# Causal attention on one core: weighing with float32 probabilities and values instead of split float16 ones

## The reference

```python
qkv = x @ W_qkv
q, k, v = jnp.split(qkv, 3, axis=-1)
q, k, v = (to_heads(q), to_heads(k), to_heads(v))      # 16 heads of 64
q, k = (apply_rope(q), apply_rope(k))
dots = jnp.einsum('bhid,bhjd->bhij', q, k) * scale
dots = jnp.where(causal, neg, dots)
attn = jax.nn.softmax(dots, axis=-1)
out = jnp.einsum('bhij,bhjd->bhid', attn, v)            # "weighing"
out = out.transpose(0, 2, 1, 3).reshape(b, n, INNER)
out = jax.nn.relu(out @ W_o1) @ W_o2
...
```

## Time and profile before

| | us |
|---|---|
| median of three runs | 5071.18 |
| profiled execution, its time | 5068.41 |
| profiled execution, its span | 5066.7 |
| `attention_heads`: stretch before the first turn | 2616 to 2722 |
| 15 turns with all side jobs (pairs 0 to 14) | 2722 to 4471 |
| last turn | 4471 to 4560 |
| both `attention_out` | 4560 to 4660 |

### The profile page before, as it was taken

The page is one execution under the profiler, slowest core; times in us unless marked ns, Lnnn a source line. Parts: engine busy times, 40 slices in busy tenths (PEclk is TensorE's granted clock), DMA queues, the critical chain, the costliest instruction groups (busy, mean ns, idle before and its releaser), DMA issues. The chain is left out here.

```text
span 5066.7 us, 84689 instructions
## 1 busy us (share of the span) xinstructions
PE 3697.3 (73%) x28907; PEld 2605.5 (51%) x28907; DVE 3704.5 (73%) x4463; ACT 2570.4 (51%) x4134; POOL 2389.1 (47%) x1532
## 2 busy tenths in 40 slices
PE   2997645555555569948936998999989898994595
PEld 1663224444434446637813665666656565663484
DVE  6993579999999989930067888888888888885101
ACT  1222456666666632222214676777767676784221
POOL 0220268888888832220034666656656666600202
PEclk9998767777777789959958999999999999996697
DMA  2000001001101000024532222222222222202254
GB/s 86 0 0 4 7 21 32 30 29 30 31 29 29 30 28 0 0 96 153 162 118 55 55 54 48 47 49 68 52 64 53 52 53 54 52 10 91 73 181 155
DMA packets 236314, 276.23 MB, mean 55 GB/s; under 512 B 63820, under 2 KB 183557, under 8 KB 234561
## 3 DMA queue, kind: packets, MB, share of 16 engines
q1 hardware_dynamic: 223056, 244.85, 17.8%
q0 software_dynamic: 8704, 24.35, 1.4%
q10 hardware_dynamic: 4224, 2.76, 0.2%
HBM read 152.60 MB, written 36.04 MB: 37 GB/s over the span
## 5 line engine op out<-in xcount | busy, mean ns | idle before, releaser
L2247 DVE TENSOR_TENSOR att_b_prob_low<-att_b_prob,att_b_prob_high 128x1024 f16<-128x1024 f32 (+2 forms) x640 | 780.4, 1220 | 64.0 <-ACT att_b_prob_high L2214 55.2
L2274 DVE TENSOR_REDUCE att_b_neg_max<-att_b_peek 128x1 f32<-128x1024 f32 (+1 forms) x748 | 667.8, 906 | 143.1 <-PE att_b_peek L2102 115.8
L2212 ACT ACTIVATE att_b_prob<-att_b_score,att_soft 128x1024 f32<-128x1024 f32 (+2 forms) x640 | 633.7, 990 | 219.9 <-PE att_b_score L2125 145.7
L1030 PE MATMUL mix_scan_hT<-ident,mix_scan_h 128*128 128x128 f32 x1024 | 248.7, 389 | 536.1 <-DVE mix_scan_h L978 502.1
L2214 ACT ACTIVATE att_b_prob_high<-att_b_score,att_soft 128x1024 f16<-128x1024 f32 (+2 forms) x640 | 630.8, 986 | 10.1 <-PE att_b_o L2153 3.6
L1030 PEld LDWEIGHTS mix_scan_hT<-ident,mix_scan_h 128*128 128x128 f32 x1024 | 172.5, 197 | 650.7 <-DVE mix_scan_h L978 443.9
L2149 PE MATMUL att_b_o<-att_b_vh,att_b_prob_high 128*128 128x65 f16 x4352 | 464.4, 195 | 36.9 <-DVE att_b_prob_low L2247 27.5
L2123 PE MATMUL att_b_score<-att_b_q_both,att_b_k_twice 128*128 128x512 f16 (+3 forms) x1280 | 450.5, 352 | 31.4 <-ACT att_b_prob_high L2214 21.9
L2149 PEld LDWEIGHTS att_b_o<-att_b_vh,att_b_prob_high 128*128 128x128 f16 x4352 | 402.4, 98 | 128.8 <-DVE att_b_prob_low L2247 73.5
L2153 PE MATMUL att_b_o<-att_b_vh,att_b_prob_low 128*128 128x65 f16 x4352 | 463.2, 194 | 0.0
L2151 PE MATMUL att_b_o<-att_b_vl,att_b_prob_high 128*128 128x64 f16 x4352 | 462.7, 193 | 0.0
(11 more groups left out here) (344 smaller groups left out, 9612.7 us busy)
## 6 DMA issues: line engine op xcount, KB each, us to landing
moe_w<-in_L_ffn_W_dram SPq DMA_DIRECT2D x64, 1024.0 KB, 8.1
mix_scan_b_row<-mix_b_rows SPq DMA_DIRECT2D x128, 256.0 KB, 3.2
att_b_crossed<-att_b_raw SPq DMA_DIRECT2D x512, 64.0 KB, 2.0
att_b_q_both<-att_b_halves SPq DMA_DIRECT2D x240, 64.0 KB, 2.0
att_b_k_twice<-att_b_halves SPq DMA_DIRECT2D x240, 64.0 KB, 2.0
moe_slots_in<-moe_route_zero SPq DMA_DIRECT2D x2, 4096.0 KB, 14.6
moe_exp_x<-moe_slots_in SPq DMA_DIRECT2D x32, 256.0 KB, 4.5
moe_slots_out<-moe_exp_y POOLq DMA_DIRECT2D x32, 256.0 KB, 6.5
```

Of the source, the lines that this page charges most:

```text
L1030: last = pe.transpose(hT_ps[:, j * D + m * P:j * D + (m + 1) * P], hs[:, b * W + m * GRP + t * P:b * W + m * GRP + (t + 1) * P], ident[:, :])
L2212: act.activation(prob[:, at:at + width], score[m % 2][:, 0:width], ACT.Exp, scale=soft[:, 0:1])
L2247: dve.tensor_tensor(prob_low[:, at:at + width], prob[:, at:at + width], prob_high[:, at:at + width], ALU.subtract).then_inc(low_ready, 1)
L2274: last = dve.tensor_reduce(neg_max[:, first + col:first + col + 1], peek_bank(kind, s)[:, base:base + nb * P], AX.X, ALU.max, negate=True)
```

## The change

Weighing is done with one float32 product a block: the probabilities are not split, and neither are the values. With that go: the second exponent of a piece on ACT, `low_part` on DVE (and with it the semaphore `low_ready`; PE's weighing now waits for `expd`), the low part of the values on DVE, and two of the three products. `prob` becomes a ring of four (`PROBS`), and ACT waits for `p_done` of four pieces before. Since four float32 pieces and float32 values do not fit beside the rest, `prob` and `headsT` lie in the first 5120 columns of X (`BORROWED`): SP stores these to DRAM (`lent`) before the tables of the rotary positions are loaded, and loads them back in the first `attention_out`, where DVE waits for them before it adds to X.

```diff
-            attention_heads(nc, ident, dram, rope, xh, xl, unit, per_unit, soft, acc, x_parked, acc_parked, name + "_b")
-            attention_outputs(nc, X, ident, dram, acc, acc_parked, name)
-
-
-def attention_outputs(nc, X, ident, dram, acc, acc_parked, name):
+            lent = nc.dram_tensor(f"{name}_lent", (P, BORROWED), F32, kind="Internal").ap()
+            attention_heads(nc, X, ident, dram, rope, xh, xl, unit, per_unit, soft, acc, x_parked, acc_parked, lent,
+                            name + "_b")
+            attention_outputs(nc, X, ident, dram, acc, acc_parked, lent, name)
+
+
+def attention_outputs(nc, X, ident, dram, acc, acc_parked, lent, name):
 
     with ExitStack() as ctx:
         earlier = ctx.enter_context(nc.sbuf_tensor(f"{name}_earlier", [P, QT * D], F32))
         fetched = nc.alloc_semaphore(name=f"{name}_fetched")
-        attention_out(nc, X, ident, dram, acc, 1, f"{name}_out1", (earlier, acc_parked, fetched))
-        attention_out(nc, X, ident, dram, earlier, 0, f"{name}_out0", None, fetched)
+        attention_out(nc, X, ident, dram, acc, 1, f"{name}_out1", ((earlier[:, :], acc_parked), (X[:, 0:BORROWED], lent)), fetched)
+        attention_out(nc, X, ident, dram, earlier, 0, f"{name}_out0", (), fetched)
...
+PROBS = 4
+BORROWED = PROBS * SPAN + 2 * GRP
...
-        vh, vl = sb("vh", [P, 2 * QT * 2 * COL], F16), sb("vl", [P, 2 * SEQ], F16)
-        v_cols = vh[:, :].rearrange("p (s e) -> p s e", e=COL)
-        prob = sb("prob", [P, 2 * SPAN])
-        prob_high, prob_low = sb("prob_high", [P, 2 * SPAN], F16), sb("prob_low", [P, 2 * SPAN], F16)
+        v = sb("v", [P, 2 * QT * 2 * COL])
+        v_cols = v[:, :].rearrange("p (s e) -> p s e", e=COL)
+        prob, headsT = X[:, 0:PROBS * SPAN], X[:, PROBS * SPAN:BORROWED]
         neg_max, max_row = sb("neg_max", [P, 2 * (QT + SB)]), sb("max_row", [QT, 2 * P], F16)
         inv = sb("inv", [P, GT])
-        heads, headsT = sb("heads", [P, QT * PAIR]), sb("headsT", [P, 2 * GRP])
+        heads = sb("heads", [P, QT * PAIR])
...
                     load_weights(0, 0)
+                    sp.dma_start(lent, X[:, 0:BORROWED]).then_inc(x_lent, 16)
                     sp.dma_start(cos[:, :], rope[0]).then_inc(tables, 16)
...
-                pe.wait_ge(low_ready, piece(t, m + 1))
+                pe.wait_ge(expd, piece(t, m + 1))
                 if g == 0:
                     pe.wait_ge(v_ready, v_count(t, V_JOBS))
                 if opens:
                     wait_unless_first(pe, o_taken, chunk_count(t if m >= 0 else t - 1, h, Q))
                 blocks = [(k, base + x * P, j + x) for k, base, j in tiles for x in range(GT - j)]
                 for k, at, i in blocks:
-                    at = slice(m % 2 * SPAN + at, m % 2 * SPAN + at + P)
+                    at = slice(m % PROBS * SPAN + at, m % PROBS * SPAN + at + P)
                     s = b * QT * 2 + k * 2 + h
                     first, final = opens and (k, i) == (blocks[0][0], blocks[0][2]), ends and k == Q * GT + i
-                    out, out_v = o_cols[:, i, :], o_cols[:, i, 0:HEAD]
-                    pe.matmul(out, prob_high[:, at], v_cols[:, s, 0:HEAD + 1], start=first, stop=False,
-                              skip_group_check=True)
-                    pe.matmul(out_v, prob_high[:, at], vl[:, s * HEAD:(s + 1) * HEAD], start=False, stop=False,
-                              skip_group_check=True)
-                    last = pe.matmul(out, prob_low[:, at], v_cols[:, s, 0:HEAD + 1], start=False, stop=final,
+                    last = pe.matmul(o_cols[:, i, :], prob[:, at], v_cols[:, s, 0:HEAD + 1], start=first, stop=final,
                                      skip_group_check=True)
                 last.then_inc(p_done, 1)
...
+                if kind == FIRST:
+                    act.wait_ge(x_lent, 16)
...
-                        .then_inc(v_high, 1)
+                        .then_inc(v_ready, 1)
...
-                at, width = m % 2 * SPAN, width_of(m)
+                at, width = m % PROBS * SPAN, width_of(m)
                 act.wait_ge(scored, piece(t, m + 1))
-                wait_unless_first(act, low_ready, piece(t, m - 1))
-                act.activation(prob[:, at:at + width], score[m % 2][:, 0:width], ACT.Exp, scale=soft[:, 0:1])
-                wait_unless_first(act, p_done, piece(t, m - 1))
-                act.activation(prob_high[:, at:at + width], score[m % 2][:, 0:width], ACT.Exp, scale=soft[:, 0:1])\
+                wait_unless_first(act, p_done, piece(t, m - PROBS + 1))
+                act.activation(prob[:, at:at + width], score[m % 2][:, 0:width], ACT.Exp, scale=soft[:, 0:1])\
                     .then_inc(expd, 1)
...
-                    if has_piece(kind, v - 1):
-                        low_part(t, v - 1)
...
-            def low_part(t, m):
-                at = m % 2 * SPAN
-                tiles = PIECES_S[m % NH][1]
-                width = tiles[-1][1] + GRP - tiles[-1][2] * P
-                dve.wait_ge(expd, piece(t, m + 1))
-                wait_unless_first(dve, p_done, piece(t, m - 1))
-                dve.tensor_tensor(prob_low[:, at:at + width], prob[:, at:at + width], prob_high[:, at:at + width],
-                                  ALU.subtract).then_inc(low_ready, 1)
...
-                elif what == "v":
-                    at = (1 - b) * QT * 2 + i * GT * 2
-                    dve.wait_ge(v_high, v_count(p, i + 1))
-                    dve.tensor_tensor(vl[:, at * HEAD:(at + GT * 2) * HEAD].rearrange("p (s d) -> p s d", d=HEAD),
-                                      side_ps[:, :].rearrange("p (s d) -> p s d", d=HEAD),
-                                      v_cols[:, at:at + GT * 2, 0:HEAD], ALU.subtract).then_inc(v_ready, 1)
...
-            if fetch:
-                sp.dma_start(fetch[0][:, :], fetch[1]).then_inc(fetch[2], 16)
+            for to, parked in fetch:
+                sp.dma_start(to, parked).then_inc(fetched, 16)
...
-            if fetched is not None:
-                act.wait_ge(fetched, 16)
+            if not fetch:
+                act.wait_ge(fetched, 2 * 16)
...
             steps = QT // GT
+            dve.wait_ge(fetched, 2 * 16)
```

More of the change, by code:

```diff
@@ L1792, in in_turns, with attention_heads @@
     turn(STREAM, 0, AFTER, PAIRS)
-def attention_heads(nc, ident, dram, rope, xh, xl, unit, per_unit, soft, acc, x_parked, acc_parked, name):
+PROBS = 4
+BORROWED = PROBS * SPAN + 2 * GRP
+def attention_heads(nc, X, ident, dram, rope, xh, xl, unit, per_unit, soft, acc, x_parked, acc_parked, lent, name):
     with ExitStack() as ctx:
@@ L1834, in attention_heads @@
                                           for n in ("crossed_over", "stacked", "shifted"))
-        w_loaded, tables, x_loaded, acc_stored, acc_cleared, wo_loaded, masks, unit_rows, w_step, w_split, qk_projected, raw_ready, rope_step, roped, v_projected, v_high, \
-            v_ready, peeked, maxed, min_ready, min_turned, row_ready, scored, expd, low_ready, p_done, \
+        w_loaded, tables, x_lent, x_loaded, acc_stored, acc_cleared, wo_loaded, masks, unit_rows, w_step, w_split, qk_projected, raw_ready, rope_step, roped, v_projected, v_ready, peeked, maxed, min_ready, min_turned, row_ready, scored, expd, p_done, \
             inv_ready, o_taken, h_turned, hT_ready, o_ready, added = map(sem, (
-                "w_loaded", "tables", "x_loaded", "acc_stored", "acc_cleared", "wo_loaded", "masks", "unit_rows", "w_step", "w_split", "qk_projected", "raw_ready", "rope_step",
-                "roped", "v_projected", "v_high", "v_ready", "peeked", "maxed", "min_ready", "min_turned", "row_ready",
-                "scored", "expd", "low_ready", "p_done", "inv_ready", "o_taken", "h_turned", "hT_ready",
+                "w_loaded", "tables", "x_lent", "x_loaded", "acc_stored", "acc_cleared", "wo_loaded", "masks", "unit_rows", "w_step", "w_split", "qk_projected", "raw_ready", "rope_step",
+                "roped", "v_projected", "v_ready", "peeked", "maxed", "min_ready", "min_turned", "row_ready",
+                "scored", "expd", "p_done", "inv_ready", "o_taken", "h_turned", "hT_ready",
                 "o_ready", "added"))
@@ L2313, in _, with attention_out @@
             dve.wait_ge(added, out_count(STREAM, 0))
-def attention_out(nc, X, ident, dram, acc, batch, name, fetch=None, fetched=None):
+def attention_out(nc, X, ident, dram, acc, batch, name, fetch, fetched):
     T0 = batch * QT
```

## The result

The changed kernel takes 5350.69 us (median of 4 runs, 5348.36 to 5357.54) beside 5069.98 us of the kernel before: a ratio of 1.055, 95% interval 1.0537 to 1.0562. The profiled execution took 5357.54 us (span 5355.9).

The account below looks back on a forecast made before the run. PE was taken to lead, DVE and ACT close behind. A turn grows 21.9 us to 138.5: 15 turns +329, last turn +24, ends +2 take the profiled 5068.4 to 5423, median 5425 us; range 5350 to 5560.

Parts of the forecast that it names:

- What goes in return: In the attention turns, PE's waits 10.4 us a turn, their tails 1.8 and low clock 2.0 were to go.
- 166 named waits: PE's waits in 15 turns, each also costing 0.16 us of hidden record end: 27 us, 1.8 a turn.
- What a block costs after: Weighing on PE: two float32 records a block at 0.112 us, 0.224 a block, 36.1 us more a turn.
- The nearest row (L722): Float32 128x128 matmul of 16 columns in the state-space stage, limited by weight load: 0.113 us a record.
- hidden loads: Rival for the weighing: records take their columns alone, 0.055 to 0.057 us; kernel faster, 5000 us; chance 0.04.
- load plus columns: Upper price of a weighing record, load and columns one behind the other: 0.168 us, 91 us a turn; no chance given.
- The check: PE's floor in a turn, float16 products 63 us, float32 side jobs 9, weighing 60.9: 133 us; forecast sum 5.5 above.
- The long wait: PE's waits at the peek for queries and keys, put down to POOL's rotations: 84.9 us in 15 turns, dropped.
- The clock: Granted clock in the turns, 0.96 of full: 2 us a turn given back; rival of half clock 7470 us, chance 0.05.
- The ring, storing X: Ring of four brings nothing more; storing X before the tables 10 us, mostly hidden, +3; reload 12.5 us, costing 0.
- The ends: Last turn +24; storing X +3 and dropped low parts of the first values -1, together +2; reload 0.
- Why all of it goes: Waits of 156.1 us in 15 turns go: ACT and DVE under half busy, PE reaching the peek 20 us later.

Follow-up runs that it names:

- the 128 columns: Changed kernel with 128 moving columns a weighing product in place of 65: 5379.44 us, 28 us above the changed kernel.
- the lighter GpSimd: Kernel before with two of GpSimd's five rotation operations a job cut to one column: 4899.65 us, ratio 0.966.
- The dummies: Changed kernel with the second exponent, the subtraction and a chain of waits like theirs put back on scratch tiles: 5363.39 us, ratio 1.0572 to the kernel before.
- the extra product: Kernel before with its third float16 weighing product made twice, 8.3 us a turn more PE work: 5120.29 us, ratio 1.0111.

## Why the prediction was right in sign and 74 us too high

A turn was forecast to grow by 21.9 us and grew by 17.3, 69 us less in 15 turns and nearly all of the miss. The traces tell where. The table counts each PE record of the 15 turns from its start to the next one's start, against the mean of its kind at the full granted clock with nothing waiting; a tail is what a record before a wait takes beyond that mean and the idle time; the low clock is the time lost in stretches at 0.50.

| us a turn | before | after | change | forecast |
|---|---|---|---|---|
| weighing | 24.7 | 59.2 | +34.5 | +36.1 |
| PE's other products | 73.3 | 72.8 | -0.5 | 0 |
| PE idle | 12.4 | 0.8 | -11.6 | -10.4 |
| tails before waits | 3.1 | 0.2 | -2.9 | -1.8 |
| low clock | 3.2 | 1.0 | -2.2 | -2.0 |
| a turn | 116.6 | 133.9 | +17.3 | +21.9 |

- *What goes in return: the step that failed.* It was sized at 10.4 + 1.8 + 2.0 = 14.2 us a turn, and 17.2 went: 1.2 more of idle time, because small waits that the sum didn't name went too; 1.1 more of tails, which were counted for 166 named waits where the trace has 286, at 0.16 us each as forecast; 0.5 of small gaps among the other products; 0.2 of clock. That is 3.0 of the 4.6 us missed.
- *What a block costs after: right in mechanism, 1.6 us a turn too high.* Two records a block, a load of 193 ns, 0.112 us a record behind the first of a step. The first costs 0.08 on the mean, since its load lies partly or wholly beside the product before it, and 40 steps a turn begin with one. The nearest row (L722) carried the price, and the 128 columns show why. The rivals by hidden loads and by load plus columns both fall.
- *The check was the better forecast.* The text worked out a floor of 133 us a turn (59.2 + 72.8 = 132.0 by the table), and its sum ended 5.5 above it without naming what would hold PE there. Nothing did. With every long wait dropped and ACT and DVE under half busy, 133 was the value to take: 5068.4 + 15 x (133 - 116.6) + 26 = 5340, and 5343 for the median. The prediction names that 5340 as one of its two ends, yet its range begins at 5350 and leaves it out.
- *The clock: right in direction.* 0.96 became 0.99. Before, 141 of the 1749 us were at 0.50, after it 33 of 2008, nearly all in three stretches behind the three longest waits left. In one of them 14 weighing records take 2.99 us, 0.214 each:

```profile
4203.03 3.19 PE L2154 MATMUL att_b_o<-att_b_v,X 128*128 128x65 f32 x14
4206.02 0.95 PE L2108 MATMUL att_b_peek<-att_b_k_twice,att_b_q_both 128*128 128x512 f16 x2
```

- *The ring, storing X: right.* Nothing. The store of 2560 KB landed in 8.8 us and the reload in 15.2, longer than the estimated 12.5, without any effect on the end (509 us from the last weighing to the end of the program, before 510):

```profile
att_lent<-X SPq DMA_DIRECT2D x1, 2560.0 KB, 8.8
...
X<-att_lent SPq DMA_DIRECT2D x1, 2560.0 KB, 15.2
```

- *The ends: nearly.* Start and last turn with end were put at +26; they are -0.6 and +21.9.
- *Why all of it goes* was half right. The long wait was ascribed to GpSimd's chain, which the lighter GpSimd bears out, and expected to be covered by PE's later arrival. The dummies show that the changed kernel's longer work covers it even beside a slow GpSimd; the extra product shows that 8.3 us a turn don't, and how much would is open. That DVE's subtraction also slows GpSimd was not in the prediction; it makes the return safe from two sides, without changing its size, since the floor caps it.

## What to carry to other kernels

When one engine is lengthened until no other can be late for it, take its floor as the time and make every microsecond above it name its cause; adding up the gains of single waits leaves out the small waits and the tails. A float32 product of 65 columns costs two weight loads here, 0.224 us, against 0.091 for three float16 products that go at the pace of their columns: one product in place of three is no saving in a chain of narrow ones. Look for a late chain's cause two engines back: here the peeks waited for a transfer, that for GpSimd, and GpSimd was slowed by a subtraction on VectorE, which made part of its lateness; a step's shift of the waiting work, or of one operation of the chain, can take the wait away, and does so only where its new place in its engine's program finds its input ready.

## What the runs showed of the hardware

- GpSimd's three two-input 128x512 float32 operations took 1592 to 1620 ns in the mean in the kernel before, beside DVE's subtraction of two tiles in SBUF, and 1267 without it; the rounding to float16 took 1913 and 1490. Inside the trace of before, the 76 of these 360 operations that overlap no subtraction took 1263 ns, the 284 that overlap one 1700, and up to 2337. The slowing goes both ways: the subtraction of 1024 columns took 1214 ns beside no work of GpSimd and 1410 beside some, up to 2296. The Trainium skill (SBUF — State Buffer, "Who interferes with whom") says that a VectorE instruction with two inputs in SBUF contends with a GpSimd instruction that reads SBUF, through a shared read interface; the trace agrees, with a stretch of 27% in the mean (1609 ns for 1267).
- Float32 records with 128x128 weights, each with its own load, stand 111.5 ns apart back to back at the full granted clock, at 65 and at 128 columns alike. A record whose load lay beside the product before it is followed after 60 ns at 65 columns and 112 at 128.
